# Two attentions and two FFNs on one core: a pair's heads in the array's two row halves, in float32r, masks first

## The chip, the cores and the metric

One Trainium2 chip, one of its cores. A program runs four phases one after the other: attention a, FFN, attention b, FFN. The metric is the device time of one execution in microseconds (us). The median of three runs before the change is 1965.94 us (1965.41 to 1966.62).

## The reference, cut to what matters

```python
x = x + attn_a(layernorm(x))      # x: 4 batches x 512 tokens x 512, float32
x = x + ffn(layernorm(x))
x = x + attn_b(layernorm(x))
x = x + ffn(layernorm(x))

# attn_a: 32 query heads of 16, 8 key/value heads (4 query heads share one), rotary embedding, no bias
# attn_b: 32 heads of 16 for q, k and v, biases
scores = einsum('bhqd,bhkd->bhqk', q, k) / 4
scores = where(causal, scores, -inf)          # 512 x 512 for each head and batch
out = softmax(scores) @ v ; out @ Wo (+ bo)
```

All inputs are float32, and the kernel keeps close to float32: where it multiplies in a shorter type, it splits each number into parts and multiplies the parts.

## The kernel before, in words

The change touches the function `attention`, which runs twice: as `aa` (phase 1) and as `ab` (phase 3). The FFN phases stay as they are.

**Pairs and steps.** The 32 heads of a batch are 16 pairs. A pair `s` takes five steps (`SUB = 5`), i = 0 to 4, and every engine walks the same list of steps. In step i TensorE makes chunk i of the pair's scores (keys down, queries across) in one of two PSUM banks (`exp_scores`, L1001), ScalarE turns it into exponentials in SBUF (L767), GpSimd zeroes what lies above the diagonal (L642). Chunks 0 and 1 are the 512 queries of the first key block of either head, chunks 2 and 3 the second and fourth key block (384 and 128 wide), chunk 4 the third key block of both heads (2 x 256). A chunk's bank is free again when its exponentials are done, so chunk i waits for chunk i-2.

**Maxima.** The softmax subtracts each row's maximum. For it TensorE computes the scores a second time two pairs ahead, queries down and keys across: blocks k = 0 to 5 (`max_scores`, L982), in steps 0, 1, 2, 3 and (two) 4, each followed by a matmul that adds the causal mask on the diagonal block (L979), in a ring of three banks. VectorE reduces each block (L867 to L871). GpSimd splits the 2 x 4 columns of maxima into three bfloat16 parts (`split_max`, L618: four instructions); one pair later, in step 2, TensorE transposes them to rows (L997), VectorE copies them (L880), and one DMA of SyncE writes them as three further rows under the queries (L571), against which the keys have ones. The pair's first scores wait for this DMA.

**Numbers.** A 16-long query or key is three bfloat16 parts, stacked six times 16 = 96 rows deep, so that one matmul of 96 (with the maxima 99) rows gives the product of all parts that matter. ScalarE makes the high part (L751 or L773) and the middle one (L781), VectorE the remainder (L856), GpSimd the low part and the copies (L674 to L676, `replicate` L647). TensorE transposes 8 heads of 128 tokens into one bank (L1104), VectorE (first part) or ScalarE (others) copies them into `stacks` (L495).

**Tasks.** Between the steps TensorE does tasks by a fixed plan (`PLAN_A`, `PLAN_B`): X transposes the normalised input, P projects it to queries, keys and values, T transposes the stacks, F transposes the context, C does so again for the output projection O. They share two PSUM banks. After step 4 of every even pair TensorE also multiplies the exponentials of four heads with the values (`values`, L1017). In `PLAN_B`, P stands at steps 0, 2, 4 and 6 of each four pairs (20 steps), T at 5, 7, 9 and 11; the last five steps hold only F. In `PLAN_A`, P is at steps 4, 9, 15, 21, 44, 49, 55 and 60 of 80, X at 40, 45, 50 and 54.

**Order on the engines.** Each engine's queue is in order. TensorE, in a step: the scores, in step 2 the transposed maxima, the maxima block, then tasks. ScalarE, in a step: what the tasks of the step before left to copy (L738 to L758: T, X, C, and of P the high part and the values), and only then the exponentials of its own step:

```python
for _, bb, u, t in table.started(region, pos, 1, "P"):       # L748
    psum = banks.read(act, where, ("P", u, t, 0))
...
act.wait_ge(scores_filled[sbk].sem, scores_filled[sbk].at(b, nth + 1))   # L766
```

## Time and profile before

| | us |
|---|---|
| median of the runs | 1965.94 |
| the profiled execution's own time | 1964.34 |
| its span, from the first to the last instruction | 1962.6 |
| TensorE (PE) busy | 1709.4, 87% |
| TensorE weight loads (PEld) busy, beside PE | 1235.3, 63% |
| VectorE (DVE) busy | 1132.9, 58% |
| ScalarE (ACT) busy | 927.3, 47% |
| GpSimd (POOL) busy | 734.2, 37% |

The profile is of one execution. Busy time counts an engine's instructions from start to end; consecutive matmuls overlap in it, so two matmuls of 0.39 us that start 0.22 us apart cost 0.22 us each, and the start times of the timeline tell what a matmul costs. DVEq, ACTq, POOLq and SPq are the queues of those engines. "<-X" behind a row names what ended an idle time.

### The profile page before, as it was taken

The numbers are of one execution on the slowest core, as the hardware profiler recorded it, in microseconds if no ns is written. First come the engines' busy times: TensorE is split into PE (matmuls) and PEld (weight loads), VectorE is DVE, ScalarE is ACT, GpSimd is POOL, SyncE is SP. The second block draws the span as 40 slices with busy tenths as digits, with TensorE's granted clock in tenths as the row PEclk, the third lists the DMA queues.
The fourth block names the chain that finished last, engine by engine and source line by source line (L and its number), as shares of the span: only waits on it lengthen the run. The fifth ranks groups of instructions, "written<-read, shape, count | busy, mean of one in ns | idle before, by whom it ended". The sixth has DMA issues, their size and how long they took to land. (4 is left out here: it accounts for less than half of the span.)

```text
span 1962.6 us, 34407 instructions
## 1 busy us (share of the span) xinstructions
PE 1709.4 (87%) x11728; PEld 1235.3 (63%) x11728; DVE 1132.9 (58%) x2474; ACT 927.3 (47%) x1740; POOL 734.2 (37%) x2278
## 2 busy tenths in 40 slices
PE   4888989889867999998489899899899967999997
PEld 4555655566535787785366666666667635777785
DVE  5777676676727654543465655665655627655543
ACT  3455555565524454531345545554554625454531
POOL 4455445454411221211445544554554511221211
PEclk8899999999987999999689999999999987999999
DMA  2000100000016211010300000001001016211010
GB/s 98 2 23 13 34 24 18 29 2 30 17 54 192 94 54 65 0 43 22 125 2 2 23 25 22 23 13 34 13 3 43 2 60 188 92 54 64 0 43 22
DMA packets 50485, 81.96 MB, mean 42 GB/s; under 512 B 10123, under 2 KB 22027, under 8 KB 50325
## 3 DMA queue, kind: packets, MB, share of 16 engines
q1 hardware_dynamic: 50324, 79.92, 13.0%
q8 instruction: 89, 1.46, 0.3%
q14 instruction: 72, 0.58, 0.1%
HBM read 62.34 MB, written 16.78 MB: 40 GB/s over the span
## 5 line engine op out<-in xcount | busy, mean ns | idle before, releaser
L247 PE MATMUL f_ring<-f_xt,f_codes 128*128 128x512 f32 (+1 forms) x1408 | 360.2, 398 | 6.4 <-DVEq L1411 5.3
L247 PEld LDWEIGHTS f_ring<-f_xt,f_codes 128*128 128x128 f32 (+1 forms) x1408 | 263.4, 188 | 76.0 <-DVEq L1411 6.1
L1269 POOL TENSOR_TENSOR f_ht<-f_work,f_ht 128x512 fp32r<-128x512 f32 (+1 forms) x88 | 114.5, 1305 | 473.2 <-ACT f_ht L1329 473.2
L767 ACT ACTIVATE ab_region<-ab_scores 128x512 f32<-128x512 f32 x320 | 184.8, 608 | 81.5 <-PE ab_scores L1013 80.2
L767 ACT ACTIVATE aa_region<-aa_scores 128x512 f32<-128x512 f32 x320 | 184.3, 599 | 81.0 <-PE aa_scores L1013 78.2
L1422 DVE TENSOR_TENSOR f_work<-f_ring,f_work 128x512 f32<-128x512 f32 (+1 forms) x176 | 120.5, 689 | 146.0 <-ACT f_work L1318 116.5
L1318 ACT ACTIVATE f_work<-f_ring,f_scales 128x512 f32<-128x512 f32 (+1 forms) x176 | 120.5, 685 | 171.6 <-PE f_ring L247 171.1
L642 POOL TENSOR_SCALAR_AFFINE_SELECT ab_region<-ab_region 128x128 f32<-128x128 f32 x512 | 136.7, 293 | 151.9 <-ACT ab_region L767 151.8
L247 PE MATMUL f_ring<-f_dcodes,f_ht 128*128 128x512 f32 (+1 forms) x704 | 177.2, 407 | 10.2 <-DVE f_down_x L1392 9.3
L642 POOL TENSOR_SCALAR_AFFINE_SELECT aa_region<-aa_region 128x128 f32<-128x128 f32 x512 | 136.5, 295 | 92.5 <-ACT aa_region L767 92.0
L247 PEld LDWEIGHTS f_ring<-f_dcodes,f_ht 128*128 128x128 f32 (+1 forms) x704 | 133.8, 193 | 48.8 <-DVE f_down_x L1392 12.8
L978 PE MATMUL aa_maxima<-aa_stacks 96*128 96x128 bf16 (+3 forms) x512 | 141.5, 311 | 22.1 <-DVE aa_nmax L871 15.7
L247 PE MATMUL ab_tasks<-ab_w,ab_xt 128*128 128x384 f32 x768 | 152.7, 347 | 4.6 <-DVE ab_bias L799 4.6
L871 DVE TENSOR_REDUCE ab_nmax<-ab_maxima 128x1 f32<-128x384 f32 (+1 forms) x256 | 148.4, 615 | 5.4 <-PE ab_maxima L979 4.2
L871 DVE TENSOR_REDUCE aa_nmax<-aa_maxima 128x1 f32<-128x384 f32 (+1 forms) x256 | 146.1, 614 | 2.6 <-PE aa_maxima L979 1.0
L978 PE MATMUL ab_maxima<-ab_stacks 96*128 96x128 bf16 (+3 forms) x512 | 137.9, 308 | 2.8 <-DVE ab_stacks L495 1.3
L247 PEld LDWEIGHTS ab_tasks<-ab_w,ab_xt 128*128 128x128 f32 x768 | 134.1, 191 | 9.4 <-issue 7.9
L1013 PE MATMUL aa_scores<-aa_stacks 99*128 99x512 bf16 (+3 forms) x512 | 124.5, 305 | 7.3 <-DMA aa_stacks<-aa_rowparts 3.6
L1013 PE MATMUL ab_scores<-ab_stacks 99*128 99x512 bf16 (+3 forms) x512 | 124.3, 304 | 6.1 <-DMA ab_stacks<-ab_rowparts 3.9
L979 PE MATMUL aa_maxima<-mask_qk,identb 128*128 128x128 bf16 x512 | 108.9, 225 | 0.0
L979 PE MATMUL ab_maxima<-mask_qk,identb 128*128 128x128 bf16 x512 | 108.1, 224 | 0.0
L856 DVE TENSOR_TENSOR ab_rest<-ab_tasks,ab_staged 128x256 f32<-128x256 f32 x64 | 27.1, 424 | 138.6 <-ACT ab_v L756 138.6
(185 smaller groups left out, 3237.2 us busy)
## 6 DMA issues: line engine op xcount, KB each, us to landing
f_x<-mid SPq DMA_DIRECT2D x32, 256.0 KB, 4.2
f_raw<-mid SPq DMA_DIRECT2D x32, 256.0 KB, 4.3
f_raw<-in_gate_q SPq DMA_DIRECT2D x10, 512.0 KB, 5.5
f_raw<-in_up_q SPq DMA_DIRECT2D x10, 512.0 KB, 4.3
f_raw<-in_down_q SPq DMA_DIRECT2D x10, 512.0 KB, 3.8
aa_x<-in_x SPq DMA_DIRECT2D x16, 256.0 KB, 2.7
aa_res<-in_x SPq DMA_DIRECT2D x16, 256.0 KB, 2.8
mid<-aa_res SPq DMA_DIRECT2D x16, 256.0 KB, 2.0
```

The source lines that it names most:

```text
L247: mm = pe.matmul(out, w, x, start=start and i == 0, stop=stop and i == len(pairs) - 1)
L642: last = pool.affine_select(out=chunk[:, at:at + P], in_=chunk[:, at:at + P], compare_op=ALU.is_ge, fill=0.0, base=0, pattern=[[1, P]], ch ...
L767: act.activation(probs[:, s // 2 % 2, SUB * (s % 2) + i, :], scores[:, sbk, :], ACT.Exp, scale=0.25).then_inc(scores_freed[sbk].sem, 1)
L856: dve.tensor_tensor(split_cols(dst), split_cols(src), staged[:, t, :, SLOT_HI, :], ALU.subtract)\
L871: last = dve.tensor_reduce(nm[:, h, qt:qt + 1], src[:, 0:(qt + 1) * P], AX_X, ALU.max, negate=True)
L978: pe.matmul(out, lhs, rhs, start=True, stop=False, skip_group_check=True)
L979: return pe.matmul(out[:, diag:diag + P], identb[:], mask[:], start=False, stop=True, skip_group_check=True)
L1013: mm = pe.matmul(scores[:, sbk, at:at + n], st[:, hk, kb * P:(kb + 1) * P], st[:, h, kb * P:T], start=True, stop=True)
L1269: pool.tensor_tensor(ht[0:r, LO, n, :], hid[0:r, n % 2, :], ht[0:r, HI, n, :].bitcast(F32), ALU.subtract).then_inc(hid_lo.sem, 1)
L1318: act.activation(scaled[0:r, j, :], src, ACT.Identity, scale=scales[0:r, j, n:n + 1])\
L1422: dve.tensor_tensor(dst, src, scaled[0:r, j, :], ALU.add)\
```

## The change

Each query and key is now two float32r parts, stacked three times 16 = 48 rows deep. The first head of a pair stands in the rows 0 to 47 and the second in 64 to 111 of the same column block, so that their matmuls use the array's row half 0 to 63 and 64 to 127. The maxima are two float32r parts, in two rows below each (48, 49 and 112, 113), written by two DMAs. `staged` and `stacks` become four-byte, four column blocks of 112 rows are transposed into a bank where there were eight of 96, and the block counts fall from 20 to 12 for 128 tokens of a unit in aa and from 16 to 8 in ab. The middle part and GpSimd's subtractions go; the high part is two ScalarE instructions (queries, keys) where it was one, and the remainder two on VectorE. The scores are made in three groups (steps 0, 2, 4), both heads' chunks in turn in both banks. The maxima blocks are made two by two in the same steps; the masks of both are put into the banks first, before the group's scores, and the maxima are added onto them. A group waits until all chunks before it are free (`SUB * s + 2 * g`). The order of ScalarE, VectorE and GpSimd and the plans stay.

```diff
-PARTS = 6
+PARTS = 3
 STK = PARTS * HD
-MAXROW = STK
-ROWS = STK + 3
+HALF = 64
+ROWS = STK + 2
+SPAN = HALF + STK
+MAXROW = 96
...
+    HQ, HK = HU // 2, KU // 2 if rep == 1 else KU
+    NST = HQ + HK
+    TPARTS = -(-NST // 4)
     STEPS = PAIRS // units
...
-        stacks = sb("stacks", [ROWS, 2, NST, T], BF16)
...
         v = sb("v", [P, VSLOTS, NT, VHEADS, VW], F32)
...
+        staged = sb("staged", [P, NT, NST, SPAN // HD, HD], F32R)
...
         var = sb("var", [P, NT], F32)
...
         MB = 6 // MAXIMA
         maxima_filled = [Signal(sem(f"maxima{i}_filled"), MB * PAIRS) for i in range(MAXIMA)]
         maxima_freed = [Signal(sem(f"maxima{i}_freed"), MB * PAIRS, 1) for i in range(MAXIMA)]
...
+            j = s % STEPS
+            h = 2 * j + i
+            return j, HQ + (j if rep == 1 else h // rep), h // rep
+        def q_cols(ap):
...
+        def k_cols(ap):
...
+            if rep == 1:
+                return ap[:, NQ:NQ + NKV].rearrange("p (j a d) -> p j a d", a=2, d=HD)
+            return split_cols(ap[:, NQ:NQ + NKV]).unsqueeze(2).broadcast_to([P, HK, 2, HD])
...
+            return staged[:, t, heads_of, c:c + 5:4, :]
         def stack_out(copy, eng, where, u, t, p):
-            n = min(8, NST - 8 * p)
-            src = banks.read(eng, where, ("T", u, t, p)).bitcast(BF16)[0:STK, 0:n * P]
-            copy(stacks[0:STK, u % 2, 8 * p:8 * p + n, t * P:(t + 1) * P],
...
+            src = banks.read(eng, where, ("T", u, t, p))[0:SPAN, 0:n * P]
...
+                for i in range(2):
+                    at = i * HALF + STK
+                    sp.dma_start(stacks[at:at + 2, unit(s) % 2, heads(s, i)[0], :].bitcast(F32),
+                                 rowparts[MAXROW + 8 * i:MAXROW + 8 * i + 8, :].bitcast(F32)).then_inc(rows_made.sem, 16)
...
+                pool.tensor_copy(np_[:, :, 0, :], nm).then_inc(nmax_hi.sem, 1)
+                pool.wait_ge(nmax_hi.sem, nmax_hi.at(b, s + 1))
+                pool.tensor_tensor(np_[:, :, 1, :], nm, np_[:, :, 0, :].bitcast(F32), ALU.subtract)\
                     .then_inc(nmax_split.sem, 1)
...
+                pool.wait_ge(qk_hi.sem, qk_hi.at(b, k + 1))
+                pool.tensor_copy(in_slot(t, slice(0, HQ), Q_AGAIN), in_slot(t, slice(0, HQ), SLOT_HI))
+                pool.tensor_copy(in_slot(t, slice(HQ, NST), K_AGAIN), in_slot(t, slice(HQ, NST), SLOT_HI))\
+                    .then_inc(replicated.sem, 1)
...
+            def high_parts(t, src):
+                act.copy(in_slot(t, slice(0, HQ), SLOT_HI), q_cols(src))
+                act.copy(in_slot(t, slice(HQ, NST), SLOT_HI), k_cols(src)).then_inc(qk_hi.sem, 1)
...
                             act.wait_ge(av_made.sem, av_made.at(b, s // 2 - 1))
-                        act.wait_ge(scores_filled[sbk].sem, scores_filled[sbk].at(b, nth + 1))
-                        act.activation(probs[:, s // 2 % 2, SUB * (s % 2) + i, :], scores[:, sbk, :], ACT.Exp,
-                                       scale=0.25).then_inc(scores_freed[sbk].sem, 1)
+                        act.wait_ge(scores_filled.sem, scores_filled.at(b, 3 * s + GROUP[i] + 1))
+                        chunk = probs[:, s // 2 % 2, SUB * (s % 2) + i, :]
+                        if i < 4:
+                            act.activation(chunk, scores[:, i % 2, :], ACT.Exp, scale=0.25)\
+                               .then_inc(scores_freed.sem, 1)
+                        else:
+                            act.activation(chunk.rearrange("p (a n) -> p a n", a=2), scores[:, :, 0:EW // 2], ACT.Exp,
+                                           scale=0.25).then_inc(scores_freed.sem, 1)
                     if rope:
                         for _, bb, u, t in table.started(region, pos, 2, "P"):
                             k = u * NT + t
                             act.wait_ge(roped.sem, roped.at(b0 + bb, k + 1))
...
+                qs, ks = slice(0, HQ), slice(HQ, NST)
+                dve.tensor_tensor(in_slot(t, qs, Q_LO), q_cols(src), in_slot(t, qs, SLOT_HI).bitcast(F32), ALU.subtract)
+                last = dve.tensor_tensor(in_slot(t, ks, K_LO), k_cols(src), in_slot(t, ks, SLOT_HI).bitcast(F32),
+                                         ALU.subtract)
+                last.then_inc(low_made.sem, 1)
+                if not rope:
+                    dve.wait_ge(low_made.sem, low_made.at(b, k + 1))
+                    dve.sem_inc(banks.is_free(where, ("P", u, t, 0)), 1)
...
+            def half(ap, i, rows):
+                return ap[i * HALF:i * HALF + rows]
+            def max_blocks(k):
+                return [(qt, P if qt == 1 else 0) for qt in ((0, 1) if k < 2 else (1 + k // 2,))]
+            def max_masks(b, s, k0):
+                for k in (k0, k0 + 1):
+                    mb, nth = k % MAXIMA, MB * s + k // MAXIMA
+                    pe.wait_ge(maxima_freed[mb].sem, maxima_freed[mb].at(b, nth))
+                    for n, (qt, at) in enumerate(max_blocks(k)):
+                        pe.matmul(maxima[:, mb, at + qt * P:at + (qt + 1) * P], identb[:], mask_qk[:], start=n == 0,
+                                  stop=False, skip_group_check=True)
...
+                st = stacks[:, unit(s) % 2]
+                for qt, at in max_blocks(k0):
+                    for k in (k0, k0 + 1):
+                        mb, i, (h, hk, _) = k % MAXIMA, k % 2, heads(s, k % 2)
+                        mm = pe.matmul(maxima[:, mb, at:at + (qt + 1) * P],
+                                       half(st[:, h, qt * P:(qt + 1) * P], i, STK), half(st[:, hk, 0:(qt + 1) * P], i, STK),
+                                       start=False, stop=True, skip_group_check=True)
+                        if qt == max_blocks(k)[-1][0]:
+                            mm.then_inc(maxima_filled[mb].sem, 1)
             def max_transposes(b, s):
...
-                    .then_inc(rows_filled.sem, 1)
-            def exp_scores(b, s, i):
-                sbk, nth = (SUB * s + i) % 2, (SUB * s + i) // 2
...
-                    pe.wait_ge(rows_made.sem, rows_made.at(b, 16 * (s + 1)))
+                pe.matmul(av[MAXROW:MAXROW + 16, 0:P], nparts[:, s % 2].rearrange("p i c q -> p (i c q)").bitcast(F32),
+                          identf[:], start=True, stop=True).then_inc(rows_filled.sem, 1)
+            def exp_scores(b, s, g):
+                pe.wait_ge(scores_freed.sem, scores_freed.at(b, SUB * s + 2 * g))
+                if g == 0:
+                    pe.wait_ge(rows_made.sem, rows_made.at(b, 32 * (s + 1)))
                 st = stacks[:, unit(s) % 2]
-                for kb, hh, at in (((0, 0, 0),), ((0, 1, 0),), ((1, 0, 0), (3, 0, 384)),
-                                   ((1, 1, 0), (3, 1, 384)), ((2, 0, 0), (2, 1, 256)))[i]:
-                    h, hk, _ = heads(s, hh)
-                    n = T - kb * P
-                    mm = pe.matmul(scores[:, sbk, at:at + n], st[:, hk, kb * P:(kb + 1) * P], st[:, h, kb * P:T],
-                                   start=True, stop=True)
-                mm.then_inc(scores_filled[sbk].sem, 1)
+                for kb, at in (((0, 0),), ((1, 0), (3, 384)), ((2, 0),))[g]:
+                    for i in range(2):
+                        h, hk, _ = heads(s, i)
+                        mm = pe.matmul(scores[:, i, at:at + T - kb * P], half(st[:, hk, kb * P:(kb + 1) * P], i, ROWS),
+                                       half(st[:, h, kb * P:T], i, ROWS), start=True, stop=True)
+                mm.then_inc(scores_filled.sem, 1)
...
+                        if i % 2 == 0:
+                            after = following(region, b, s, 2)
+                            if after is not None:
+                                max_masks(*after, i)
+                            exp_scores(b, s, i // 2)
+                            if after is not None:
+                                if after[1] % STEPS == 0:
+                                    banks.all_emptied(pe, where, [("T", unit(after[1]), t, p)
+                                                                  for t in ((0, 1), (2,), (3,))[i // 2]
+                                                                  for p in range(TPARTS)])
+                                max_scores(*after, i)
                         if i == TRANSPOSE_AT and (after := following(region, b, s, 1)) is not None:
...
-                        out = banks.take(pe, where, ("T", u, t, p)).bitcast(BF16)
-                        for h in range(min(8, NST - 8 * p)):
-                            src = staged[:, t, 8 * p + h].rearrange("p s d -> p (s d)")
-                            mm = pe.transpose(out[0:STK, h * P:(h + 1) * P], src, identb[:])
+                        out = banks.take(pe, where, ("T", u, t, p))
+                        for h in range(min(4, NST - 4 * p)):
```

## Rows read from the trace of the kernel before

**Rows 1.** The page, span and part 1.
```profile
span 1962.6 us, 34407 instructions
...
PE 1709.4 (87%) x11728; PEld 1235.3 (63%) x11728; DVE 1132.9 (58%) x2474; ACT 927.3 (47%) x1740; POOL 734.2 (37%) x2278
```

**Rows 2.** Busy time by stretch, aa and ab (the header names the columns).
```profile
core 0: us, PE busy (x) PEld busy (x) DVE busy (x) ACT busy (x) POOL busy (x), PEclk, DMA share, GB/s
50.00:556.00 506.00, 450.78 (x3864) 289.60 (x3864) 358.18 (x921) 276.33 (x518) 251.34 (x945) 0.96 0.06 20
...
991.00:1587.00 596.00, 541.53 (x4704) 389.44 (x4704) 345.95 (x837) 313.64 (x679) 304.33 (x1135) 0.99 0.06 18
```

**Rows 3.** Waits of PE in 50 to 556: us in total, times, longest.
```profile
PE aa_maxima L978 <- DVE aa_nmax L871: 15.7, 24, 1.4
PE aa_av L997 <- POOL aa_nparts L632: 14.4, 18, 2.3
```

**Rows 4.** Waits of PE in 991 to 1587.
```profile
PE ab_av L997 <- POOL ab_nparts L632: 10.0, 15, 2.3
```

**Rows 5.** Timeline of PE, a pair with no P or T (start, us, instruction).
```profile
1214.52 0.39 PE L1013 MATMUL ab_scores<-ab_stacks 99*128 99x512 bf16 x1
1214.74 0.22 PE L978 MATMUL ab_maxima<-ab_stacks 96*128 96x128 bf16 x1
...
1215.79 0.39 PE L1013 MATMUL ab_scores<-ab_stacks 99*128 99x384 bf16 x2
1216.11 0.23 PE L997 MATMUL ab_av<-identb,ab_nparts 128*24 128x128 bf16 x1
1216.27 0.34 PE L978 MATMUL ab_maxima<-ab_stacks 96*128 96x384 bf16 x1
1216.44 0.22 PE L979 MATMUL ab_maxima<-mask_qk,identb 128*128 128x128 bf16 x1
1216.50 0.60 PE L1038 MATMUL ab_tasks<-identf,ab_avs 128*128 128x128 f32 x4
...
1218.72 0.38 PE L1013 MATMUL ab_scores<-ab_stacks 99*128 99x512 bf16 x1 [0.40 <-DMA ab_stacks<-ab_rowparts]
```

**Rows 6.** Groups by line and form, weight loads: count, busy us, mean ns.
```profile
L247 PEld LDWEIGHTS f_ring<-f_xt,f_codes 128*128 128x128 f32 x1280 | 242.8, 190 | 67.0 <-DVEq L1411 6.1 <-DVE f_work L1422 4.0
...
L1013 PEld LDWEIGHTS ab_scores<-ab_stacks 99*128 99x128 bf16 x512 | 42.6, 99 | 30.1 <-issue 13.6 <-ACT ab_region L767 12.9
...
L247 PEld LDWEIGHTS f_ring<-f_ht,f_da 128*64 128x64 f32 x160 | 21.3, 134 | 14.1
```

**Rows 7.** Timeline of PE around a P at step 0.
```profile
1186.89 0.34 PE L247 MATMUL ab_tasks<-ab_bias,ab_sel 128*128 128x384 f32 x1
1187.07 0.39 PE L1013 MATMUL ab_scores<-ab_stacks 99*128 99x512 bf16 x1
...
1187.59 0.38 PE L1013 MATMUL ab_scores<-ab_stacks 99*128 99x384 bf16 x2
```

**Rows 8.** Timeline of ACT around the same P.
```profile
1187.27 0.37 ACT L751 CAST ab_staged<-ab_tasks 128x256 bf16<-128x256 f32 x1 [2.12 <-PE ab_tasks L247]
1187.54 0.34 ACT L756 COPY ab_v<-ab_tasks 128x64 f32<-128x64 f32 x2
1187.74 1.12 ACT L767 ACTIVATE ab_region<-ab_scores 128x512 f32<-128x512 f32 x2
```

**Rows 9.** Timeline of DVE in a late stretch of aa.
```profile
248.85 1.28 DVE L871 TENSOR_REDUCE aa_nmax<-aa_maxima 128x1 f32<-128x512 f32 x2
```

**Rows 10.** Timeline of PE in the same stretch.
```profile
248.88 0.38 PE L1013 MATMUL aa_scores<-aa_stacks 99*128 99x512 bf16 x1 [0.36 <-DMA aa_stacks<-aa_rowparts]
```

**Rows 11.** SyncE's DMA of the maxima rows, by line.
```profile
L571 SPq DMA_DIRECT2D ab_stacks<-ab_rowparts x64: 698/698/827, 991.8 to 1580.5; - x64
```

**Rows 12.** Timeline of PE, the values of one quad.
```profile
307.01 2.35 PE L1030 MATMUL aa_av<-aa_region,aa_v 128*17 128x512 f32 x32
```

**Rows 13.** Timeline of DVE in the pair of rows 5.
```profile
1216.41 0.23 DVE L880 COPY ab_rowparts<-ab_av 24x128 bf16<-24x128 bf16 x1
```

More of the change, by code:

```diff
@@ L386, in attention @@
     HI, LO = 0, 1
-    SLOT_HI, SLOT_MID, Q_LO, K_LO = 2, 3, 5, 1
+    SLOT_HI, Q_AGAIN, Q_LO, K_LO, K_AGAIN = 0, 1, 2, 1, 2
     with ExitStack() as ctx:
@@ L691, in _ @@
         def _(act):
-            for sems in (banks.freed, [f.sem for f in scores_freed + maxima_freed]):
+            for sems in (banks.freed, [scores_freed.sem], [f.sem for f in maxima_freed]):
                 for one in sems:
@@ L772, in part @@
                             act.wait_ge(roped.sem, roped.at(b0 + bb, k + 1))
[L773 to L782 removed]
+                            high_parts(t, rest[:, k % 2, :])
             whole(act, part)
```

145 lines of the change are left out of this document (38 added, 107 removed).

## The prediction

> **What bounds the kernel now.** I read the page's first part, then the busy time by stretch, the waits, and the timelines of single pairs. The two attentions are the stretches of 506 and 596 us, 1102 of the span's 1962.6 us; nothing of the FFNs changes. PE is busy 89% and 91% of them, DVE 71% and 58%, ACT 55% and 53%, at a granted clock of 0.96 and 0.99 [rows 1, 2]. So PE's stream is the bound, but not everywhere: a pair takes 506/64 = 7.9 us in aa and 596/64 = 9.3 in ab, but of the gaps between the first scores of consecutive pairs in the timeline 24 are under 5.4 us (14 in aa, with a mean of 4.6, and 10 in ab, all 4.2 as in [rows 5]). They are odd pairs with little but their own work, and there a chain sets the time: transposed maxima at 1216.11, VectorE's copy at 1216.41 for 0.23, the DMA, and the next pair's scores at 1218.72, whose last idle time the DMA ended [rows 5, 13]. In aa PE also waits for VectorE's reductions, and in both for GpSimd's split maxima, 14.4 and 10.0 us [rows 3, 4].
>
> **Term 1, PE's stream.** Start to start, a bf16 matmul of 512, 384 and 128 columns takes 0.22, 0.17 and 0.06 us [rows 5]; 256 lie between at 0.11. A head's scores are 512, 384, 256 and 128 wide, 0.56 us, its maxima the same, so a pair has 2.24 us of them beside 0.48 us of masks, which stay. After, the two heads may run side by side, which halves the stream. But weights are now four bytes: a load of 128 columns has 190 ns against 99 for bf16, of 64 columns 134 [rows 6], so it holds the loader (190-134)/64 = 0.87 ns per column, 0.11 us for 128. A round of both heads needs two loads. If the loads too go side by side, the four rounds take 0.22+0.17+0.11+0.11 = 0.61 us; if one follows the other, 4 x 0.22 = 0.88. Nothing in the trace shows row halves. Its nearest row is the values: 16 float32 products in four column quarters, as 32 instructions, take 2.35 us [rows 12], with 5120 columns in all, 0.46 ns per column, no more than a bf16 column costs, though a 128-wide float32 transpose costs 0.11 us, twice that [rows 5]. So quarters do overlap. I take the middle, 0.75 us, for scores and for maxima: -0.74 us per pair.
>
> Entering and leaving another shape of the array costs. After the two scores of 384 and 128 (0.23) the 24-column transpose should start at 1216.02; it starts at 1216.11, and the next full matmul 0.16 after it where 0.06 is its width [rows 5]: 0.1 us each way. Three groups a pair enter and leave the halves; one of the six falls together with a switch that exists: +0.5 us (0 to 0.6). The transposed maxima become a float32 product of two instructions of 0.11 instead of 0.06: +0.15. Per pair -0.74+0.5+0.15 = -0.09 us. Bounds: loads side by side and no switch cost, 2 x 0.61 - 2.24 + 0.15 = -0.87; halves not side by side, each round twice as long (2 x 2 x 0.61 = 2.44 us), with switches 0.20+0.5+0.15 = +0.85. Over the 104 other pairs: -9 us (-90 to +88).
>
> By the Trainium skill, TensorEngine Tiling (Array Packing), section Key Properties, changing the tiling mode drains TensorE; the 0.1 us each way above agree. TensorE: Matmul & The Clock Gate, section Weight-path perf modes, says that 128 weights load fast unless they are FP32: the trace agrees with 99 against 190 ns, and this speaks against the change. By the same page's section Measured speedup vs the span model (four row tiles, 3.07 times) an estimate for two tiles is 2.24/(2 x 0.77) = 1.46 us, beside my 1.5.
>
> **Term 2, T.** 640 transposes in aa at 0.06 become 384 at 0.11 (the four of L1038 take 0.60 with one's 0.28 latency [rows 5]); 1024 in ab become 512: 38+61 = 99 us become 42+56 = 98. Nothing. ScalarE's copy out of the bank gets half as wide and takes less; VectorE's stays. Nobody waits much for either.
>
> **Term 3, ScalarE behind P.** ScalarE does P's copies in the step after it and only then that step's exponentials. Before, chunk 1 and its maxima come after P on PE, and the scores of step 2 need chunk 0 alone: they start at 1187.59, 0.52 us after P's end at 1187.07, with PE full [rows 7]. After, both chunks are made before P, and step 2 needs chunk 1 free. Its exponentials are behind P's high part and values: high part 0.20 after P's end, 0.27 for it (0.33 as two), 0.20 for the values' two copies, then 0.60 for the exponentials [rows 8]: 1.4 us, in which PE has only two masks (0.12). The wait is 1.3 us for each P at a pair's step 0 or 2. In ab those are P 0 and 2 of each four-pair unit, 15 units: 30 x 1.3 = 39. In aa P at 15, 55, 60, ten times, with only a value copy in front and sometimes a T beside: 10 x 0.8 = 8; X at 40, 45, 50, nine times 0.5 = 4. Together +51 (25, if half is hidden, to 65).
>
> **Term 4, the light pairs.** Their gap is now step 0 to step 2, then the chain. Step 2 needs both chunks free: scores 0.4, two exponentials 1.1, a signal: 1.6 us, and in odd pairs, as these are, the context's copy is ahead, +0.2. Then scores and maxima of the group 0.4 to 0.5. Then the chain, 1218.72-1216.11 = 2.61 us, plus the second DMA behind the first, 0.70 us of SyncE [rows 11], plus 0.15 for the float32 product. That is 5.6 us. Against 4.2 in ab (10 pairs) and 4.6 in aa (14 pairs): +14+14 = +28 (12, if the second DMA costs nothing and the groups half as much, to 40). GpSimd's shorter split (two instructions for four) saves nothing here, since the product now comes later than the split.
>
> **Term 5, masks ahead of scores.** The masks of the next pair's first two blocks need block 4 reduced; before, the scores came first and the block behind them needed only block 3. At 248.85 VectorE starts on blocks 4 and 5, while PE starts the scores at 248.88 [rows 9, 10]: block 4 would end at 249.53, and scores come 0.9 us later. aa has 24 waits of this kind already [rows 3]; 30 x 0.4 = +12 (0 to 30), ab nothing.
>
> **Term 6, GpSimd.** Of the 24.4 us of waits for split maxima [rows 3, 4] most lie in light pairs; elsewhere -3.
>
> **Sum.** -9+0+51+28+12-3 = +79 us on the profiled execution's 1964.3: 2043. The median lies 1.6 above it: 2045 us.
>
> **Rivals.** (a) Faster. PE's stream at its lower bound, both streams and loads side by side and switches free, -90, with terms 3 to 6 at their lower ends, 25+12+0-3 = 34: -56, 1910 us. For it: PE is busy nine tenths. Against: the 0.1 us of a switch are in the trace, and the wait for both banks is in the code. It decides when the stream saves more per pair (104 of them) than the waits put back: above 0.85 us against my 88 us of waits, above 0.33 against 34. (b) The halves do not run side by side: the matmuls of 48 rows take as long as those of 96 did, with slower loads. Term 1 is +88 instead of -9; I let some 20 of the 97 fall into the new waits: 2045+97-20 = 2122. For it: nothing in the trace shows halves. Against: the quarters overlap. (c) Stream and waits cancel within 0.2%, 3.9 us, which is about what a measurement can tell: -88 from the stream against the 88 us of waits, 1966.
>
> **Chances.** My forecast 0.62, own range 1995 to 2090; (a) 0.16; (b) 0.18; (c) 0.04. The range for all, 1945 to 2125, leaves out the best of (a) and the worst of (b). Faster 0.15, same 0.04, slower 0.81.
>
> **What would show it.** In the changed kernel's timeline two scores of a group start almost together (forecast) or 0.22 us apart (b); the rounds' spacing gives the loads, the first matmul after a group the switch. PE's waits for ScalarE's exponentials should reach some 50 us, all behind P at a pair's step 0 or 2; the waits for the rows' DMA should grow, with no gap between pairs under 5.2 us. The FFN stretches must keep their 320 us. If those waits stay under 20 us the forecast is wrong in terms 3 and 4; if PE's scores and maxima take 1.2 us a pair and nothing is lost at the switches, in term 1.

## The result, and the profile after

| | before | after |
|---|---|---|
| median | 1966.28 us, 4 runs (1965.41 to 1967.32) | 2199.17 us, 4 runs (2196.40 to 2201.71) |
| ratio | | 1.1184, 95% interval 1.1165 to 1.1203 |
| span, mean granted clock | 1962.6 us, 0.948 | 2198.1 us, 0.889 |

The change makes the kernel 233 us slower. I forecast slower, but by 79, and the time lies 74 us above the range.

First the page of the changed kernel, as [rows 1] of before:

```profile
span 2198.1 us, 32570 instructions
...
PE 1842.3 (84%) x11088; PEld 1312.7 (60%) x11088; DVE 1165.0 (53%) x2570; ACT 876.7 (40%) x1740; POOL 539.9 (25%) x1640
```

PE has 640 instructions fewer and 133 us more busy time. Busy time by stretch, each attention from its first scores to its last (columns: stretch and length, then busy time of PE, PEld, DVE, ACT, POOL, then the granted clock); it answers to [rows 2]:

```profile
60.50:668.00 607.50, 510.12 (x3667) 326.93 (x3666) 366.06 (x933) 261.69 (x517) 185.43 (x702) 0.86 0.05 17
1110.30:1817.30 707.00, 592.49 (x4267) 420.74 (x4266) 359.26 (x889) 281.99 (x678) 193.59 (x766) 0.91 0.05 15
```

Cut the same way, the kernel before has 496.7 us at 0.97 and 591.5 at 0.99. So aa is 111 us longer and ab 116; all the rest of the span has 9. Now the waits of PE in aa (window 55 to 665) and in ab (1090 to 1815), for [rows 3, 4]:

```profile
PE aa_maxima L986 <- DVE aa_nmax L868: 51.2, 67, 2.0
PE aa_scores L1018 <- ACT aa_region L771: 15.1, 25, 1.2
PE aa_maxima L986 <- DVE aa_nmax L865: 13.6, 24, 1.3
```

```profile
PE ab_scores L1018 <- ACT ab_region L771: 42.2, 43, 1.2
PE ab_maxima L986 <- DVE ab_nmax L868: 20.4, 44, 1.2
...
PE ab_maxima L986 <- DVE ab_nmax L865: 7.1, 13, 0.6
```

L986 is the masks, now ahead of the scores, waiting for a reduced bank: 65 us in aa, 28 in ab. L1018 is the scores waiting for exponentials: 57. Before, aa had 20.6 us of the first kind (15.7 of them in [rows 3]) and 3.3 of the second, ab about one of either.

The timeline of PE around a P at a pair's step 0, and of ACT beside it, for [rows 7, 8]:

```profile
1337.21 0.50 PE L1018 MATMUL ab_scores<-ab_stacks 50*128 50x512 f32 x2
1337.55 0.39 PE L995 MATMUL ab_maxima<-ab_stacks 48*128 48x128 f32 x4
1337.87 2.38 PE L249 MATMUL ab_tasks<-ab_w,ab_xt 128*128 128x384 f32 x12
1340.09 0.34 PE L249 MATMUL ab_tasks<-ab_bias,ab_sel 128*128 128x384 f32 x1
1340.27 0.29 PE L986 MATMUL ab_maxima<-mask_qk,identb 128*128 128x128 bf16 x2
1341.69 0.50 PE L1018 MATMUL ab_scores<-ab_stacks 50*128 50x384 f32 x4 [1.13 <-ACT ab_region L771]
1342.03 0.39 PE L995 MATMUL ab_maxima<-ab_stacks 48*128 48x384 f32 x2
1342.35 0.39 PE L1005 MATMUL ab_av<-identf,ab_nparts 128*16 128x128 f32 x2
```

```profile
1340.47 0.27 ACT L717 CAST ab_staged<-ab_tasks 128x128 fp32r<-128x128 f32 x1 [2.05 <-PE ab_tasks L249]
1340.63 0.27 ACT L718 CAST ab_staged<-ab_tasks 128x128 fp32r<-128x128 f32 x1
1340.79 0.35 ACT L760 COPY ab_v<-ab_tasks 128x64 f32<-128x64 f32 x2
1340.99 0.64 ACT L771 ACTIVATE ab_region<-ab_scores 128x512 f32<-128x512 f32 x1
```

Two things happened as forecast. From the first of the two scores to the maxima behind them is 0.34 us for both heads' 512 columns, where one head's took 0.22, and in the trace the second of two such matmuls starts 0.003 us after the first: the halves run side by side. And P's end (1340.27) is 1.42 us ahead of the next scores (1341.69), with ScalarE's four instructions between.

Another place of the same kernel, again a P, this one with its wait; below it the stretch of that P by `--windows`, its granted clock third from the end:

```profile
1245.62 0.44 PE L986 MATMUL ab_maxima<-mask_qk,identb 128*128 128x128 bf16 x2
1247.08 0.79 PE L1018 MATMUL ab_scores<-ab_stacks 50*128 50x384 f32 x4 [1.02 <-ACT ab_region L771]
1247.67 0.63 PE L995 MATMUL ab_maxima<-ab_stacks 48*128 48x384 f32 x2
1248.23 0.61 PE L1005 MATMUL ab_av<-identf,ab_nparts 128*16 128x128 f32 x2
1248.76 4.21 PE L249 MATMUL ab_tasks<-ab_w,ab_xt 128*128 128x384 f32 x12
```

```profile
1248.70:1252.80 4.10, 4.10 (x14) 4.02 (x13) 0.85 (x2) 0.00 (x0) 0.52 (x2) 0.50 0.01 2
```

The same twelve matmuls take 4.21 us instead of 2.38: the granted clock is 0.50, so TensorE is at 1.2 GHz here, not at 2.4 as at 1337 us (1.00). The forecast has no such term.

### The profile page after: what moved, and what is told of

Its sections match the earlier page's. It is cut to its first block and busy times, and to the rows that moved or that the text cites. A ratio compares the mean times of both kernels' runs of the same rounds, so it can differ in the third digit from the quotient of the medians.

```text
span 2198.1 us, 32570 instructions
## 1 busy us (share of the span) xinstructions
PE 1842.3 (84%) x11088; PEld 1312.7 (60%) x11088; DVE 1165.0 (53%) x2570; ACT 876.7 (40%) x1740; POOL 539.9 (25%) x1640
## 5 line engine op out<-in xcount | busy, mean ns | idle before, releaser
L771 ACT ACTIVATE ab_region<-ab_scores 128x512 f32<-128x512 f32 x256 | 147.7, 607 | 105.6 <-PE ab_scores L1018 104.2
L771 ACT ACTIVATE aa_region<-aa_scores 128x512 f32<-128x512 f32 x256 | 143.8, 596 | 101.9 <-PE aa_scores L1018 99.1
L249 PE MATMUL ab_tasks<-ab_w,ab_xt 128*128 128x384 f32 x768 | 173.8, 381 | 4.6 <-DVE ab_bias L797 4.6
L986 PE MATMUL aa_maxima<-mask_qk,identb 128*128 128x128 bf16 x512 | 87.9, 243 | 68.0 <-DVE aa_nmax L868 51.6
L1018 PE MATMUL ab_scores<-ab_stacks 50*128 50x512 f32 (+3 forms) x512 | 94.7, 408 | 45.3 <-ACT ab_region L771 44.1
L1018 PE MATMUL aa_scores<-aa_stacks 50*128 50x512 f32 (+3 forms) x512 | 101.7, 436 | 17.6 <-ACT aa_region L771 16.6
L986 PEld LDWEIGHTS aa_maxima<-mask_qk,identb 128*128 128x128 bf16 x512 | 43.8, 104 | 113.1 <-DVE aa_nmax L868 67.1
L848 DVE TENSOR_TENSOR ab_staged<-ab_tasks,ab_staged 128x128 fp32r<-128x128 f32 x64 | 18.7, 292 | 165.1 <-ACT ab_v L760 164.6
L1111 PE MATMUL ab_tasks<-identf,ab_staged 128*112 128x128 f32 x512 | 85.7, 300 | 21.7 <-DVE ab_ctx L888 7.9
L986 PE MATMUL ab_maxima<-mask_qk,identb 128*128 128x128 bf16 x512 | 76.0, 235 | 29.4 <-DVE ab_nmax L868 20.4
```

The source lines that it names most:

```text
L249: mm = pe.matmul(out, w, x, start=start and i == 0, stop=stop and i == len(pairs) - 1)
L771: act.activation(chunk, scores[:, i % 2, :], ACT.Exp, scale=0.25)\
L848: dve.tensor_tensor(in_slot(t, qs, Q_LO), q_cols(src), in_slot(t, qs, SLOT_HI).bitcast(F32), ALU.subtract)
L986: pe.matmul(maxima[:, mb, at + qt * P:at + (qt + 1) * P], identb[:], mask_qk[:], start=n == 0, stop=False, skip_group_check=True)
L1018: mm = pe.matmul(scores[:, i, at:at + T - kb * P], half(st[:, hk, kb * P:(kb + 1) * P], i, ROWS), half(st[:, h, kb * P:T], i, ROWS), start ...
L1111: mm = pe.transpose(out[0:SPAN, h * P:(h + 1) * P], src, identf[:])
```

## The experiments

Every kernel was timed beside the kernel before on the same chip, so "over" is the difference of these two medians. Clock and length are of aa and ab, from first to last scores.

| kernel | us | over | aa: us, clock | ab: us, clock |
|---|---|---|---|---|
| before | 1966.3 | 0 | 496.7, 0.97 | 591.5, 0.99 |
| the change | 2199.2 | 232.9 | 607.5, 0.86 | 707.0, 0.91 |
| b5_groups (before, the order alone) | 2157.2 | 195.0 | 582.3, 0.90 | 694.9, 0.97 |
| c1_scores (before, scores' order) | 2077.2 | 112.2 | 535.2, 0.96 | 660.5, 0.99 |
| c2_maxima (before, maxima's order) | 2028.4 | 63.4 | 529.9, 0.96 | 615.6, 0.98 |
| c3_behind (b5, masks behind) | 2143.4 | 178.5 | 573.3, 0.91 | 687.6, 0.98 |
| a1_act (change, P's copies later) | 2163.8 | 201.6 | 613.6, 0.85 | 665.6, 0.92 |
| a2_masks (change, masks behind) | 2293.7 | 331.5 | 625.5, 0.85 | 787.0, 0.86 |
| a6_onedma (change, one rows DMA) | 2199.4 | 234.8 | 615.8, 0.84 | 692.9, 0.93 |
| a4_full (change, no halves) | 2217.5 | 255.3 | 625.1, 0.90 | 716.0, 0.98 |
| a7_fill (change, fillers) | 2232.6 | 267.6 | 610.1, 0.95 | 720.9, 0.97 |
| e1_full_fill (fillers, no halves) | 2269.7 | 304.6 | 625.4, 0.99 | 761.2, 0.98 |
| a8_half (change, half-array fillers) | 2240.4 | 273.3 | 637.3, 0.87 | 723.3, 0.94 |
| a9_whole (change, whole-array fillers) | 2332.3 | 365.1 | 679.1, 0.89 | 767.7, 0.96 |
| d1_busy (before, fillers at the starts) | 1992.7 | 25.6 | 498.9, 0.97 | 591.3, 0.99 |
| d2_busy (before, fewer of them) | 1957.7 | -7.4 | 496.5, 0.97 | 594.6, 0.98 |

**The order without the numbers: b5_groups.** The kernel before with the change's lists of steps:

```diff
-                        exp_scores(b, s, i)
-                        ahead, ks = MAXIMA_AT[i]
...
-                                max_scores(*after, k)
+                        if i % 2 == 0:
+                            after = following(region, b, s, 2)
+                            if after is not None:
+                                max_masks(*after, i)
+                            exp_scores(b, s, i // 2)
...
+                                max_scores(*after, i)
```

> The kernel before (its bf16 parts, 96 rows, one DMA for the maxima's rows) with the change's order of work alone: both heads' scores in one group at a pair's steps 0, 2 and 4, both banks waited for, the masks put into the maxima's banks ahead of the group's scores. No row halves, no float32 product. Theory W: the order alone brings the waits and with them the lower clock: most of the 233 us, 2080 to 2200 us, with the granted clock of the attention stretches at 0.93 or less. Theory H: only the waits' own time comes, the clock stays at 0.96 or more and the time is 2000 to 2070 us, and the rest of the 233 us is of the row halves or the float32 parts. The wait for ScalarE's exponential behind P should be in it at 1 to 1.5 us each in either theory.

195 us come with the order alone, against 233 with the whole change. The time is theory W's, but its reason holds in aa only, where the clock went from 0.97 to 0.90; ab has 103 us more at 0.97, as H has it.

**The two parts of the order: c1_scores and c2_maxima.** One takes the scores in groups and leaves the maxima as they were, the other the reverse.

> The kernel before with the scores' half of the change's order alone: both heads' scores in one group at a pair's steps 0, 2 and 4 with both banks waited for; the maxima stay one head at a time at steps 0 to 4, each mask behind its scores. The kernel before with the whole order took 2157 us, 195 more than before; in its profile PE waited 66 us for ScalarE's exponentials. Theory A (the wait for both banks is the larger part): 2060 to 2110 us, with a wait for ScalarE's exponential of 50 to 70 us and the granted clock of the second attention at 0.97 or more. Theory B (the masks ahead of the scores and the maxima in pairs are the larger part): 2000 to 2050 us.

> The kernel before with the other half of the change's order alone: maxima of both heads at steps 0, 2 and 4, their masks put into the banks ahead of that step's scores; the scores stay one head at a time, each waiting for its own bank. Theory A: 2000 to 2050 us. Theory B (masks ahead of scores, maxima in pairs): 2060 to 2110 us, with PE waiting 70 to 90 us for VectorE's reductions as in the kernel with the whole order (86 us), most of it in the first attention, whose clock would be at 0.93 or less. My forecast of the change had 12 us for this half.

112 and 63 us, both in theory A's ranges; their sum is 176, and together they cost 195. The waits of PE in aa, of c1_scores and then of c2_maxima:

```profile
PE aa_scores L1017 <- ACT aa_region L770: 53.4, 77, 2.5
PE aa_scores L1017 <- ACT aa_region L773: 6.1, 7, 0.9
```

```profile
PE aa_maxima L985 <- DVE aa_nmax L871: 42.7, 67, 1.6
PE aa_maxima L985 <- DVE aa_nmax L868: 15.5, 27, 1.4
```

With ab's 62 us, c1_scores has 122 us of waits for ScalarE in 166 places. Theory A expected 50 to 70, for I had counted P's alone. By the trace some 129 of the 166, with 91 us, have none of P's value copies within the 2 us before them; in 45 of these 91 us the exponential waited for stands right behind a copy of T's bank, in 30 right behind another exponential. A place in aa of the first kind, PE and then ACT:

```profile
92.94 0.42 PE L1109 MATMUL aa_tasks<-identb,aa_staged 128*96 128x128 bf16 x4
94.23 0.61 PE L1017 MATMUL aa_scores<-aa_stacks 99*128 99x512 bf16 x2 [0.87 <-ACT aa_region L773]
```

```profile
92.32 0.46 ACT L787 CAST aa_staged<-aa_rest 128x320 bf16<-128x320 f32 x1 [1.37 <-DVE aa_rest L862]
92.68 1.00 ACT L496 COPY aa_stacks<-aa_tasks 96x1024 bf16<-96x1024 bf16 x1
93.59 0.59 ACT L773 ACTIVATE aa_region<-aa_scores 128x512 f32<-128x512 f32 x1
```

**ScalarE's order: a1_act.** The change, with P's copies behind the exponentials at odd steps:

```diff
-                    for _, bb, u, t in table.started(region, pos, 1, "P"):
...
+                    odd = step is not None and step[2] % 2 == 1
+                    if not odd:
+                        projected()
...
+                    if odd:
+                        projected()
```

> The change, with one thing moved: at a pair's odd steps ScalarE makes its exponentials first and copies P (its high parts and its values) behind them; at even steps as in the change. So P no longer stands between a group's scores and their exponentials where a P ends at an odd step. Theory W (waits let TensorE's clock fall, and the fallen clock makes the rest longer): the wait for ScalarE's exponential behind P goes in part or whole, 57 us of it stand in the profile of the change, the granted clock of the two attention stretches rises from 0.86 and 0.91 by 0.01 to 0.04, and the time falls by more than the wait that goes: to 2100 to 2160 us. Theory H (the matmuls of half the rows let the clock fall, whatever the waits): the clock stays at 0.86 and 0.91 and the time falls by the waits alone, to 2140 to 2180 us. If ScalarE's copies are late for the tile's later work instead, the wait shows up under another line and the time stays within 10 us of 2199.

31 us less: the time is theory H's, and the wait behind P is real. In ab the waits at the scores' line fall from 44 to 11 us over the whole trace and the stretch from 707 to 666 us; the clock moves by 0.01. In aa nothing is gained (613.6 us), for there the waits behind ScalarE were 17 us in all and are now 14.

**Masks behind the scores: a2_masks and c3_behind.** The same edit in the change and in b5_groups:

```diff
-                            if after is not None:
-                                max_masks(*after, i)
                             exp_scores(b, s, i // 2)
                             if after is not None:
+                                max_masks(*after, i)
```

> The change, with the masks put back behind the group's scores: a group issues its scores, then its masks, then the scores on top of them. So a group's scores no longer wait for VectorE's reduction of the maxima; the masks do, later. In the profile of the change PE waits at the masks' line for VectorE's reduction 65 us in the first attention stretch and 27 us in the second. Forecast term of masks ahead of scores was 12 us. Theory W: those waits shrink by half, the clock rises a little, time 2130 to 2180 us. Theory H: time 2160 to 2190 us at the same clock. If the waits only move (the reduction is late in any order, because the group before it came late), the time stays within 10 us of 2199.

> The kernel before with the change's whole order, except that a group's masks come behind its scores (2157 us with the masks ahead). In the change itself the same edit made the time 94 us longer (2294 against 2199 us). Theory S (in the change the edit put full-array masks between two half-array groups, so that the row mode switches twice more in a group): here there are no halves, so the time does not rise: 2110 to 2160 us, less of the wait for VectorE's reductions. Theory M (the order is bad by itself: the scores reach their wait for ScalarE sooner and the masks' stay becomes longer): it rises here too, to 2190 to 2250 us.

In the change it costs 99 us more, without halves it saves 17. Both of a2_masks's expectations were wrong, theory S of c3_behind holds. The timeline of a2_masks shows the price of a switch:

```profile
1367.45 0.50 PE L1018 MATMUL ab_scores<-ab_stacks 50*128 50x512 f32 x2
1367.88 0.40 PE L986 MATMUL ab_maxima<-mask_qk,identb 128*128 128x128 bf16 x4
1368.21 0.50 PE L995 MATMUL ab_maxima<-ab_stacks 48*128 48x128 f32 x4
1368.64 3.06 PE L249 MATMUL ab_tasks<-ab_w,ab_ct 128*128 128x512 f32 x12
```

The two scores take 0.43 us to the next instruction, where they took 0.34 ahead of other half-array work; the maxima 0.43 for 0.32. So a switch out is 0.1 us, and each group has one more pair of switches: 384 groups x 0.2 = 77 us of the 99. By the split of the next section it is 66 us of work and 53 of a lower clock (0.86 for 0.91 in ab), less 21 of waits.

The two kernels without halves say more. c3_behind takes 178.5 us over the kernel before and c1_scores 112.2. They differ in that c3_behind also makes the maxima two by two: 66 us. b5_groups differs from c3_behind only in the place of the masks: 17 us.

**The second DMA: a6_onedma.** Left out are the second head's maxima; the exponential's scale is 0.001.

```diff
-                for i in range(2):
+                for i in range(1):
                     at = i * HALF + STK
```

> The change with one DMA for the maxima's rows instead of two: the second head's rows are not written (its exponentials get no maximum, and the exponential's scale is 0.001 to keep the numbers in range). My forecast put 0.70 us for the second DMA into each of 24 light pairs, 17 us of the 233. Theory D (the chain through the DMA sets the light pairs): the gap of the light pairs falls from 5.6 to 4.9 us and the time by 15 to 20 us, to 2180 to 2185 us. Theory V (VectorE's reductions set them, since the masks ahead of the scores wait for these: the kernel before with the order alone has one DMA and the same 5.6 us): the gap stays at 5.6 and the time within 8 us of 2199.

Theory V: 2 us from the change's 233 (aa 8 longer, ab 14 shorter, at clocks 0.01 and 0.02 apart), and the light pairs of ab keep 5.6 us. This is why, in the change's own timeline of such a pair:

```profile
1141.76 0.50 PE L1018 MATMUL ab_scores<-ab_stacks 50*128 50x512 f32 x2
...
1143.43 0.50 PE L1018 MATMUL ab_scores<-ab_stacks 50*128 50x384 f32 x4
...
1144.09 0.39 PE L1005 MATMUL ab_av<-identf,ab_nparts 128*16 128x128 f32 x2
...
1146.55 0.28 PE L986 MATMUL ab_maxima<-mask_qk,identb 128*128 128x128 bf16 x2 [0.32 <-DVE ab_nmax L868]
1147.15 0.29 PE L986 MATMUL ab_maxima<-mask_qk,identb 128*128 128x128 bf16 x2 [0.31 <-DVE ab_nmax L868]
1147.40 0.50 PE L1018 MATMUL ab_scores<-ab_stacks 50*128 50x512 f32 x2
```

The last wait before the next scores is the masks', for VectorE, not the DMA's. The masks' wait is not the whole of the gap: in ab it is 4.2 us before, 4.9 in c1_scores, 5.0 in c2_maxima, 5.3 in c3_behind with the masks behind, and 5.6 in b5_groups.

**The halves: a4_full.** Both heads' matmuls contract rows from 0 up; the separation of the heads is left out, and the exponential's scale is 0.001.

```diff
             def half(ap, i, rows):
 
-                return ap[i * HALF:i * HALF + rows]
+                return ap[0:HALF + rows]
```

> The change, but every one of the score and maxima matmuls contracts the rows from 0 up (112 or 114 of them) for both heads, not its own half: so no two lie side by side in the array's row halves, and the array's row mode is not switched. This leaves out the separation of the two heads (both get the sum of both), and the exponential's scale is 0.001 to keep the numbers in range. Order, waits and numbers of instructions are those of the change. Theory H (matmuls of half the rows let the clock fall): the granted clock of the two attention stretches comes back to 0.95 or more (before: 0.97 and 0.99; the change: 0.86 and 0.91), and the time comes out below 2199 although the rounds of a group, about 1.3 us longer in sum for each pair, are no longer side by side. Theory W (the waits do it): the groups are longer on TensorE, by about 1.5 us a pair or 150 us in all at most, part of which fills what were waits, the clock stays within 0.03 of the change's or rises a little since TensorE is busier, and the time is 2230 to 2350 us. If the halves were never side by side, the time stays at 2199 within 20 us.

Neither theory as written. The clock did come back, to 0.90 and 0.98, partly as H has it, but the time rose by 22 us (18 between the medians themselves). That is near what halves which never lay side by side would give, but here two scores of 512 columns take 0.54 us at a granted clock of 1.00, for 0.34 in the change. So the halves save only 22 us net, and with them the clock is lower. The waits don't explain that: in ab, from first to last scores, PE has 115 us of them at 0.98 here and 113 at 0.91 in the change.

**Fillers: a7_fill and e1_full_fill.** Additional matmuls whose results are overwritten, ahead of the masks; e1_full_fill has them together with a4_full's edit.

```diff
                     pe.wait_ge(maxima_freed[mb].sem, maxima_freed[mb].at(b, nth))
+                    for _ in range(4):
+                        pe.matmul(maxima[:, mb, 0:P], identb[:], mask_qk[:], start=True, stop=True,
+                                  skip_group_check=True)
```

> The change, with four more mask matmuls of 128 columns per maxima bank, ahead of the masks (their result is overwritten): eight a group, 24 a pair, some 0.06 us each at the full clock and 0.11 at half, so 1.4 to 2.6 us of work for TensorE a pair, 90 to 165 us in an attention of 64 pairs if all of it were on the path. Theory C (a good part of the time comes from a clock that falls where PE idles): the granted clock of the attention stretches rises from 0.86 and 0.91 by 0.03 or more, and the time rises by less than 100 us, to 2200 to 2290 us. Theory N (the clock follows the row halves, not the idle time): the clock moves by less than 0.02 and the time rises to 2330 to 2500 us.

> The change with the fillers ahead of the masks (2233 us, clock 0.95 and 0.97) and, as in a4_full, every score and maxima matmul over rows from 0 up, so that no two lie side by side; this leaves out the separation of the two heads, and the exponential's scale is 0.001. Without the fillers the pair differed by 18 us (2199 with the halves, 2217 without) at unlike clocks (0.86 and 0.91 with, 0.90 and 0.98 without). If the halves' gain was eaten by the clock, then at like clocks it shows: 2290 to 2370 us here, 60 to 140 more than with the halves, against a working of 1.3 us a pair or 166 us in all if all of it were on the path. If it was eaten by waits of the group, this comes within 30 us of 2233.

3072 matmuls more (172 us at the 0.056 that 128 columns take from start to start at the higher clock) and 35 us of time: theory C, with the clock up by 0.09 and 0.06. The clearest row is P's product, identical work in every kernel. By line and form: the kernel before, the change, a7_fill (count, busy us, mean ns):

```profile
L247 PE MATMUL ab_tasks<-ab_w,ab_xt 128*128 128x384 f32 x768 | 152.7, 347 | 4.6 <-DVE ab_bias L799 4.6
```

```profile
L249 PE MATMUL ab_tasks<-ab_w,ab_xt 128*128 128x384 f32 x768 | 173.8, 381 | 4.6 <-DVE ab_bias L797 4.6
```

```profile
L249 PE MATMUL ab_tasks<-ab_w,ab_xt 128*128 128x384 f32 x768 | 154.2, 349 | 4.6 <-DVE ab_bias L797 4.6
```

21 us of busy time in this one group, and 9 in aa's (80.3 to 89.5), are the clock alone; the fillers give back 20 and 7 of them. A unit's first pair in ab, where most of the low clock lies, went from 16.3 to 15.2 us with 24 matmuls more in it, while the next two went from 10.0 and 8.5 to 11.0 and 9.4. With fillers in both, the halves are worth 37 us (304.6 less 267.6, between the two ranges), against 22 without. The clocks are nearer each other than before, but not alike, 0.95 and 0.97 against 0.99 and 0.98, so this doesn't yet settle what the clock took of the gain; the split in the next section does more.

**Half-array fillers: a8_half and a9_whole.** Four matmuls per scores bank ahead of each group's scores, of 48 rows in the bank's own row half, or of all 128.

> The change, with four extra matmuls of 48 rows by 128 columns per scores bank in front of each group's scores (bank i's in row half i; their result is overwritten). To be compared with the next kernel, the same but with whole 128-row ones. Theory R (half-array work counts for less with TensorE's clock): the granted clock of the attention stretches stays within 0.03 of the change's 0.86 and 0.91 although TensorE is busier, and the time rises by 60 us or more. Theory C (only the idle time matters): the clock rises as with the whole-array fillers (to 0.93 and more) and the time is that of the next kernel within 20 us.

> The change, with four extra matmuls of 128 rows by 128 columns per scores bank in front of each group's scores (their result is overwritten). With such fillers ahead of the masks the time was 2233 us and the granted clock 0.95 and 0.97 in the two attentions. Both theories: 2210 to 2260 us here, clock 0.93 or more.

This pair failed as a test. Half-array fillers raised the clock by 0.01 and 0.03, whole ones by 0.03 and 0.05, which leans to R; but the half-array ones cost 40 us of time and the whole ones 132, so the load isn't the same, and 40 us is less than R's 60. Behind the wait for ScalarE the whole ones took little from the waits (84 and 113 us from first to last scores, for 95 and 113), which is why I was wrong on their time.

**TensorE busy at the starts of the parts: d1_busy and d2_busy.** The kernel before with transposes of the identity ahead of its long waits:

```diff
+def keep_busy(pe, out, identf, n):
+    for _ in range(n):
+        pe.transpose(out[:, 0:P], identf[:], identf[:])
...
         out = self.ring.take(pe, b, f"X{t}")
+        keep_busy(pe, out, self.identf, busy)
         pe.wait_ge(self.normed.sem, self.normed.at(b, t + 1))
```

> The kernel before (not the change), with TensorE kept busy by transposes of the identity while it waits at the start of each attention and each feed-forward part: their results are overwritten. There the granted clock is 0.5 in the profile of the kernel before, from about 30 to 58 us, 583 to 616 us and 930 to 995 us, and the work that follows the waits runs at half the speed (P's twelve matmuls 4.18 us where 2.25 us is usual). Theory C (idle time lets the clock fall): the clock there goes to 1.0 and the time falls by 8 to 25 us, to 1940 to 1957 us. If the clock isn't set by idle time, or if the path in these stretches is not TensorE's: within 5 us of 1965.

> The kernel before with TensorE kept busy at the start of each part, as in d1_busy, with fewer fillers. d1_busy had the clock at 0.97 over the span (0.95 before) and took 26 us more: in its profile a hundred fillers of 0.13 us began only when the part's semaphores let them, at 597.49 us, and ran 13.05 us, past the moment at which the normalised tile was there, in each of the four parts. Here they end before it by that profile: 38 in a feed-forward part, 28 and 8 in the attentions, and 4 to 10 in shorter waits. Expected: the clock near 0.96 and 1945 to 1965 us; slower than 1967 would say that these stretches are not TensorE's at any clock.

d1_busy is 26 us slower: its hundred fillers begin late and end 6 to 12 us after the normalised tile is there. d2_busy, with 287 fillers in all, is the fastest kernel of the study, ratio 0.9962 (0.9946 to 0.9979), a gain of 0.4%. PE in both, at the start of ab: the kernel before, then d2_busy:

```profile
958.94 4.18 PE L247 MATMUL ab_tasks<-ab_w,ab_xt 128*128 128x384 f32 x12 [4.59 <-DVE ab_bias L799]
```

```profile
950.31 2.95 PE L247 MATMUL ab_tasks<-identf 128*128 128x128 f32 x25 [0.43 <-DVE ab_xt L939]
954.49 2.32 PE L253 MATMUL ab_tasks<-ab_w,ab_xt 128*128 128x384 f32 x12 [1.23 <-DVE ab_bias L805]
```

## Why the prediction was wrong

The sign was right. The miss is 154 us. By the experiments, the order was forecast at 91 us (terms 3, 4 and 5) and is 195; the arithmetic (terms 1, 2 and 6) was forecast at -12 and is +38 (233 less 195).

A second split asks what kind of time came. From each trace I added up PE's idle times of over 0.15 us (waits) and took the rest of the span as work. Where the granted clock is at the lower of its two levels, half of the work's time is put down to the clock. P's twelve matmuls take 4.01 us from start to start at the lower level and 2.22 at the higher, so half is somewhat too much, and the last column an upper estimate.

| kernel, us | span | waits | work as at the higher clock | added by the lower clock |
|---|---|---|---|---|
| before | 1963 | 243 | 1659 | 61 |
| c1_scores | 2073 | 317 | 1681 | 75 |
| c2_maxima | 2026 | 278 | 1670 | 78 |
| c3_behind | 2143 | 357 | 1675 | 111 |
| b5_groups | 2159 | 356 | 1686 | 117 |
| the change | 2198 | 344 | 1667 | 187 |
| a1_act | 2161 | 312 | 1666 | 183 |
| a2_masks | 2295 | 323 | 1733 | 240 |
| a4_full | 2219 | 332 | 1777 | 110 |
| a7_fill | 2222 | 275 | 1838 | 109 |
| e1_full_fill | 2272 | 271 | 1935 | 67 |

The work column can be tested: a7_fill has 171 us more of it than the change, and its fillers are 172 by their number; a1_act, which moves work of ScalarE alone, has the change's within 2 us.

So of the 235 us between the two spans 101 are waits, 8 are work and 126 the lower clock. The forecast had 88, -9 and nothing. **That is the step that failed:** every term was priced as if TensorE kept the higher clock.

**The missing mechanism: the granted clock.** By the windows, 2 x (1 - clock) x length, TensorE spends 170 us of aa and 127 of ab at the lower level, against 30 and 12 before. The order alone brings part of it (117 against 61 in the table), the arithmetic more (187). It is also why the two parts of the order cost more together than apart: 112 + 63 became 195, and in the table the sum of the two misses the whole by 4 us in the waits, by 6 the other way in the work and by 25 in the clock. The split is bookkeeping, not an experiment: at the higher clock PE would come to some waits sooner and wait longer there. But a7_fill shows that the clock can be bought back: 171 us more work, 69 less of waits and 78 less of clock. Without the clock's part the order would still be dear: it costs ab 103 us at 0.97.

What lowers the clock is only partly shown. In aa the order alone does it, with waits of at most 1.6 us each: 0.90 in b5_groups against 0.97. The Trainium skill has such a case (TensorE: Matmul & The Clock Gate, section A second HAM failure mode: psum-queue depth-cycling): frequent short idle times between groups of matmuls make the clock go back and forth. In aa the traces agree: the granted level changes 15 times before, 27 times in b5_groups and 45 in the change; fillers bring the change's clock to 0.95, with 17. In ab the same order leaves the clock at 0.97 with 126 us of waits, and the halves bring it to 0.91 with 113. Whether half-array matmuls lower it by themselves, or by leaving TensorE less work between its waits, stays open.

**Term 5 and what it left out.** Masks ahead of scores were forecast at +12, and the place of the masks is worth 17 us (b5_groups less c3_behind). What had no price is the maxima two by two, 66 us (c3_behind less c1_scores). A group needs two banks of three reduced where one block needed one: in the change PE waits for VectorE's reductions 91 times in aa and 57 in ab, where I had 24 in aa, times a delay, and "ab nothing". In c2_maxima, where both stand together, the cost is 63 us, and ab has 22 us of such waits. A resource that is in use before and asked for earlier after has to be walked through every group, not scaled from its present waits.

**Term 3 failed in its count: +51, "ScalarE behind P".** The single stretch from P's end to the next scores is right to 0.02 us (1.42 against 1.4), and a1_act shows that it is this. But the wait for both chunks also bites where ScalarE is behind T's or the context's copies, or where TensorE has less than two exponentials' time of work between groups. The scores' order alone costs 112 us, where terms 3 and 4 have 79. The sentence of the forecast that all these waits would be behind P is wrong; in the change their sum (57 us) is near the forecast's 50 because the masks' wait in front hides part of them: without halves they are 66 us with the masks ahead (b5_groups) and 134 with the masks behind (c3_behind).

**Term 4, the light pairs: right number, partly by luck.** 5.6 us was forecast and is there in ab; in aa it is mostly 6.2 to 6.5. The parts of the forecast in fact add up to 5.7. The second DMA, 0.70 of it, is worth nothing (a6_onedma); without it the sum is 5.0. VectorE's reductions end the gap.

**Term 1: right in the work, and its gain went to the clock.** Scores and maxima of a pair take 0.34 + 0.32 + 0.34 + 0.32 + 0.22 + 0.33 = 1.87 us, and the switch into the halves lies in the spacing of the masks before them, three times 0.1: 2.2 in all, against 2.0 forecast and 2.24 before. Rival (b), halves not side by side, is out. In the table the change has 19 us less work than b5_groups, where terms 1, 2 and 6 have -12, and a4_full, without the halves, has 91 more, where (b) has +88. So the halves do save 110 us of work (1777 less 1667). But the clock takes back 77 and the waits 12, and 22 are left. And 38 us came where -12 stood, because the clock took 70.

**Terms 2 and 6** can't be told apart in these runs; no run isolates them.

## What to carry to other kernels

Where a reordering makes an instruction wait for two things instead of one, or for an older one, list for every step what the producer has in its queue at that time; the sum over the kinds of step I did not look at was larger than the one that I did. And where PE is busy nine tenths and the bound, price idle time above its own length: what follows it can run at half the clock, so a saving in the stream is not a saving if it is spent waiting. Here the halves saved 110 us of work and brought 22.

## What the runs showed of the hardware

- Two float32r matmuls of 50 rows and 512 columns in different row halves of the array start 0.003 us apart, and the next work starts 0.34 us after the first; over 114 rows each (a4_full) two such take 0.54, and one bf16 matmul of 512 takes 0.22. An additional boundary between half-array and whole-array work costs 0.1 us each way (a2_masks).
- Work added to TensorE can be nearly free or even speed its surroundings: 172 us of fillers for 35 us of time ahead of the masks (a7_fill), the same 172 us behind the wait for 132 us (a9_whole), 48 us of them in the parts' first waits and 7 us less (d2_busy). The place decides.
- Fillers that outlive the wait which they bridge cost time: 6 to 12 us too late in each of four parts, 26 us in all (d1_busy).
- The granted clock can be lower at equal waits: in ab 0.98 with 115 us of waits (a4_full), 0.91 with 113 when the same matmuls lie in row halves (the change).
